# A decoder block in float32 on one core: the first feed-forward group rewoven with cross-attention steps and output tiles

## What is computed

```python
h = LN(x)                                   # causal self-attention, 16 heads of 32
s = (q @ k.T + slope * (key - query)) / sqrt(32)
s = 30 * tanh(s / 30)
x = x + softmax(causal(s)) @ v @ Wo.T + bo
h = LN(x)                                   # cross-attention, one head of 512
s = where(mask, h @ ctx.T / sqrt(512), -1e30)
x = x + softmax(s) @ ctx                    # zero for a batch entry without a valid token
h = LN(x)                                   # feed-forward, 512 -> 1536 -> 512
gate = silu(h @ fp8(gate_w) * gate_scale)
up = h @ fp8(up_w) * up_scale
x = x + (gate * up) @ fp8(down_w) * down_scale
```

## Time and profile before

| | us |
|---|---|
| median of 3 runs | 593.75 |
| lowest, highest | 592.24, 596.52 |
| the profiled execution | 594.02 |
| its span, first to last instruction | 592.3 |

### The profile page before, as it was taken

The page is one execution under the profiler, slowest core; times in us unless marked ns, Lnnn a source line. Parts: engine busy times, 40 slices in busy tenths (PEclk is TensorE's granted clock), DMA queues, the critical chain, the costliest instruction groups (busy, mean ns, idle before and its releaser), DMA issues.

```text
span 592.3 us, 9934 instructions
## 1 busy us (share of the span) xinstructions
PE 553.8 (94%) x3890; PEld 454.0 (77%) x3890; DVE 337.2 (57%) x674; ACT 242.6 (41%) x471; POOL 280.0 (47%) x284
## 2 busy tenths in 40 slices
PE   2998998999989999897779999999999999999997
PEld 2787786888768887686657888888888888888885
DVE  6578648874498645975637855335533456234322
ACT  3538863578534774435543343023320334023310
POOL 5657867846757458794665322013410243003320
PEclk9999998999999999998999999999999999999999
DMA  8862132532217220219562802000001000000001
GB/s 267 298 183 73 38 107 72 173 114 72 72 37 213 73 73 18 74 55 316 163 231 73 265 1 90 35 37 1 2 18 54 0 1 1 35 37 0 2 18 53
DMA packets 44189, 50.98 MB, mean 86 GB/s; under 512 B 3184, under 2 KB 25712, under 8 KB 44144
## 3 DMA queue, kind: packets, MB, share of 16 engines
q1 hardware_dynamic: 44144, 50.36, 26.0%
HBM read 36.72 MB, written 13.63 MB: 85 GB/s over the span
## 4 chain that ended last, share of the span: by engine, by line
PE 75%; POOL 10%; ACT 6%; DVE 5%; issue 2%; DMA 1%; SPq 0%; DVEq 0%; ACTq 0%
PE bank L262 49%; PE bank L396 15%; PE bank L257 3%; PE bank L318 2%; POOL probs L625 2%; PE bank L336 2%; POOL x_res L646 2%; PE bank L343 2%; POOL q_w L634 2%; POOL q_w L632 2%; PE bank L354 1%; DVE q_m L1060 1%; ACT probs L785 1%; POOL reduced L619 1%; ACT probs L780 1%
## 5 line engine op out<-in xcount | busy, mean ns | idle before, releaser
L262 PE MATMUL bank<-reduced 128*128 128x512 f32 x1536 | 363.0, 394 | 1.6 <-DVE reduced L990 1.6
L262 PEld LDWEIGHTS bank<-reduced 128*128 128x128 f32 x1536 | 287.5, 189 | 64.2 <-issue 3.6
L729 POOL TENSOR_TENSOR f_parts<-fused,f_parts 128x512 fp32r<-128x512 f32 x48 | 62.2, 1296 | 178.3 <-ACT f_parts L920 178.3
L902 ACT ACTIVATE tanh_g<-bank,half_gate 128x512 f32<-128x512 f32 x48 | 33.1, 690 | 156.0 <-PE bank L262 155.6
L396 PE MATMUL bank<-reduced,f_parts 128*128 128x512 f32 x384 | 88.7, 391 | 0.0
L396 PEld LDWEIGHTS bank<-reduced,f_parts 128*128 128x128 f32 x384 | 71.9, 188 | 15.3 <-issue 0.5
L625 POOL TENSOR_SCALAR_AFFINE_SELECT probs<-probs 128x512 f32<-128x512 f32 x64 | 41.6, 679 | 66.7 <-ACT probs L785 66.7
L1176 DVE SCALAR_TENSOR_TENSOR silu<-tanh_g,bank 128x512 f32<-128x512 f32 x48 | 32.9, 685 | 61.0 <-ACT tanh_g L902 61.0
L780 ACT ACTIVATE probs<-bank 128x512 f32<-128x512 f32 x64 | 33.0, 603 | 54.5 <-PE bank L318 51.7
L632 POOL TENSOR_TENSOR q_w<-q_w,q_m 128x512 f32<-128x512 f32 x36 | 47.2, 1310 | 3.1 <-DVE q_m L1062 3.1
L634 POOL TENSOR_TENSOR q_w<-q_w,q_m 128x512 f32<-128x512 f32 x36 | 47.2, 1310 | 2.8
(11 more groups left out here) (86 smaller groups left out, 537.0 us busy)
## 6 DMA issues: line engine op xcount, KB each, us to landing
quantized<-q_w SPq DMA_DIRECT2D x36, 256.0 KB, 3.3
reduced<-quantized SPq DMA_DIRECT2D x12, 512.0 KB, 7.8
memT_sb<-in_memT SPq DMA_DIRECT2D x16, 256.0 KB, 4.6
mem_sb<-in_mem SPq DMA_DIRECT2D x16, 256.0 KB, 5.6
out<-y_sb SPq DMA_DIRECT2D x16, 256.0 KB, 2.0
x_res<-in_x SPq DMA_DIRECT2D x3, 1024.0 KB, 6.8
q_w<-in_gate_w SPq DMA_DIRECT2D x12, 256.0 KB, 3.2
q_w<-in_up_w SPq DMA_DIRECT2D x12, 256.0 KB, 3.2
```

What stands on the lines that cost most here:

```text
L262: ins = pe.matmul(dst, stationary, moving, start=(n == 0), stop=(n == len(pairs) - 1))
L729: pool.tensor_tensor(f_lo[:, f, :], fused[:, f % 2, :], f_hi[:, f, :].bitcast(F32), ALU.subtract).then_inc(f_lo_ready, 1)
```

## The change

- PE: after slices 0 and 1 there is one loop over the slices 2 to 11. Each turn is a slice, a step of cross-attention (of group 2 until f = 6, of group 3 from f = 7) and, in turns 3 to 6, one output tile. Slice 1 goes into banks 5 and 3 instead of 4 and 5. In turns 4 to 7 the pair of banks is reversed, so that the up half takes the bank that the output tile of the turn before used. The last steps of cross(3, .) move between the halves of the down tiles; `down` can now do a part of its slices.
- DVE, ACT and POOL: the same loop. The late slabs (prepare 34, 35; round 33 to 35; flag 32 to 35) are spread over the turns, one a turn, behind `fuse`, `high` and `ffn_low`. `norm_moments` and `norm_apply` of group 3 follow right behind its last output tile.
- The flag sum goes to bank 5 instead of bank 7, and DVE adds it to `fuse_c` before its four `x_low`, not behind them.
- SyncE: in group 3 the first four `load_gate_up` come two slab steps earlier, followed by the loads of cross-attention's memory for group 2.

The diff, cut (in `down` and in the SyncE part all edits are shown):

```diff
-F_BANK = 7
+F_BANK = 5
...
             gate_up(0, 0, (0, 1))
             cross(G - 2, 0)
-            gate_up(0, 1, (4, 5))
+            gate_up(0, 1, (PT_BANK, RO_BANK))
             context(G - 1, 3)
             cross(G - 2, 1)
-            gate_up(0, 2, (0, 1))
-            cross(G - 2, 2)
-            gate_up(0, 3, (6, 7))
-            cross(G - 2, 3)
-            for i in range(GT):
-                wo_proj(G - 1, i, (0, 1, 6, 7)[i])
-                if i < GT - 1:
-                    cross(G - 2, 4 + i)
-            gate_up(0, 4, (0, 1))
-            gate_up(0, 5, (6, 7))
-            for k in range(6):
-                gate_up(0, 6 + k, ((0, 1), (6, 7))[k % 2])
-                cross(G - 1, k)
+            for f in range(2, FT):
+                pair = ((0, 1), (6, 7))[f % 2]
+                gate_up(0, f, pair[::-1] if 4 <= f < 8 else pair)
+                if f < 7:
+                    cross(G - 2, f)
+                else:
+                    cross(G - 1, f - 7)
+                if 3 <= f < 7:
+                    wo_proj(G - 1, f - 3, (6, 0)[f % 2])
...
-                        turn_x3(g + 1, i, (2, 4, 0, 1)[i] if g == 0 else i)
...
+                        turn_x3(g + 1, i, (2, 0, 1, 5)[i] if g == 0 else i)
+                if g == 0:
+
+                    down(0, 0, 6, 0, DOWN_FIRST)
+                    cross(G - 1, 5)
+                    down(0, 1, 7, 0, DOWN_FIRST)
+                    cross(G - 1, 6)
+                    down(0, 0, 6, DOWN_FIRST)
+                    down(0, 1, 7, DOWN_FIRST)
+                    down(0, 2, 2)
+                    down(0, 3, 4)
...
-                    if hg == 1 and g:
+                    slabs = slabs_at(ROUNDED, g, hg)
+                    if hg == 0 and g == G - 1:
+                        slab_steps(slabs[:2])
+                        slabs = slabs[2:]
+                        wait_filled(sp, ("V", g, GT - 1))
+                        for f in range(4):
+                            load_gate_up(f)
+                    if hg == (0 if g == G - 1 else 1) and g:
                         for i in range(GT):
                             load_memT(g - 1, i)
...
             ffn_low(0, 0)
+            low_part(G - 1, 3)
+            ffn_low(0, 1)
             flag_slabs(flagged[:1])
             round_slabs(late[:1])
...
+            for f in range(2, FT):
                 ffn_low(0, f)
-                if f == 7:
+                flag_slabs(flagged[f - 1:f])
+                round_slabs(late[f - 1:f])
+                if f == 6:
+                    norm_scale(1, G - 1)
...
+            for f in range(2, FT):
+                gate(0, f)
+                if f == 2:
+                    context_high(G - 1, 3)
+                if f < 7:
+                    cross(G - 2, f)
+                else:
+                    cross(G - 1, f - 7)
+                high(0, f)
+                flag_slabs(late[f - 2:f - 1])
...
             fuse(0, 0)
-            prepare_slabs(late[:1])
             fuse(0, 1)
             normalize_context(G - 1, 3)
             cross(G - 2, 1)
-            prepare_slabs(late[1:])
...
+            for f in range(2, FT):
+                fuse(0, f)
+                if f < 7:
+                    cross(G - 2, f)
+                else:
+                    cross(G - 1, f - 7)
+                if 3 <= f < 7:
+                    wo_out(G - 1, f - 3)
+                prepare_slabs(late[f - 2:f - 1])
+                if f == 6:
+                    norm_moments(1, G - 1)
+                    norm_apply(1, G - 1, G - 1)
```

More of the change, by code:

```diff
@@ L385, in turn_x3, with down @@
                 transposes(dst, xn2[:, i, :]).then_inc(done, 1)
-            def down(g, i, b):
-                dst, done = take(("D", g, i), b)
+            def down(g, i, b, first=0, last=FT):
+                if first == 0:
+                    take(("D", g, i), b)
+                dst, done = bank[b], filled[b]
                 t = slice(i * S, (i + 1) * S)
-                for f in range(FT):
+                for f in range(first, last):
                     if i == 0:
@@ L473, in _ @@
                     for i in range(GT):
[L474 to L478 removed]
+                        turn_x3(g + 1, i, (2, 0, 1, 5)[i] if g == 0 else i)
[9 more added lines that the diff above has]
+                else:
+                    for i in range(GT):
+                        down(g, i, 4 + i)
         @block.sync
@@ L563, in _ @@
                             load_mem(g - 1, i)
-                    if g == G - 1 and hg == 1:
-                        wait_filled(sp, ("V", g, GT - 1))
-                        for f in range(4):
-                            load_gate_up(f)
                     if g == G - 1 and hg == 3:
@@ L1145, in _ @@
                 prepare_slabs(slabs_at(PREPARED, g, 2))
-                for i in range(GT):
-                    x_low(g + 1, i)
                 if g == G - 1:
@@ L1153, in _ @@
                     wait_drained(dve, ("F",))
+                for i in range(GT):
+                    x_low(g + 1, i)
                 normalize_context(g, 2)
```

70 lines of the change are left out of this document (12 added, 58 removed).

## The result

| | before | after |
|---|---|---|
| median (6 runs each) | 593.71 us | 581.14 us |
| lowest, highest | 592.24, 596.88 | 578.59, 583.00 |
| the profiled execution | 594.02 | 580.64 |
| its span | 592.3 | 578.9 |

After over before is 0.977 (95% interval 0.975 to 0.980). The medians are 12.6 us apart; the spans of the two profiled executions 13.4 us.

The account below looks back on a forecast made before the run. PE's work was taken as the floor, so only its idle or low-clock time could go: 2.35 + 1.26 + 3.50 + 4.19 + 1.6 = 12.9 us gained, 0.3 given back, 594.0 - 12.6 = 581.4 us; range 578.5 to 588.0.

Parts of the forecast that it names:

- the clock terms: Time at low clock won back behind two stops: 1.26 us at context(3, 2), 1.6 us behind cross(2, 2)'s turned probabilities.
- What bounds the kernel: PE's work is the floor; some 10 us of its idle time lie in the stretch's first 51 us.
- Term 1: Flag in bank 5, added first: the 2.35 us stop ahead of context(3, 2) goes, plus 1.26 us of clock.
- Term 2: Scores of cross(2, 1): slice 1 leaves bank 4 and the slab goes behind slice 2; all 3.50 us go.
- Term 3: Turned probabilities of cross(2, 2): the exp comes in time, so 4.19 us go, plus 1.6 us of clock.
- The new waits: Waits the new turns add on PE: 0.2 to 0.3 us at group 3's norm, nothing at the other places listed.
- ring through POOL: In turns 2 to 4 POOL's four instructions take 5.2 us; the slice held back is 16 us away: no wait.
- Rival A: One stop forms anew, 2 to 3 us plus 1.6 us of clock: 585.4 us; chance 0.20 with the flag's failure.
- B: The stops only change place, about 3 us in each of turns 3 to 6: 593.4 us; chance 0.08.
- C: POOL and DVE hold each other up, 5.3 us in turns 3 to 5 plus clock falls: 602 us; chance 0.04.
- The clock's rule: Half rate is TensorE's default and activity releases it; with the stops gone no clock fall is left.
- the rows alone: Judged by the profile's rows, a clock fall could come in the same place without the stop; 1.3 us would stay.

Follow-up runs that it names:

- the change again: The changed kernel itself, unaltered, measured once more as a yardstick: 580.74 us, ratio to before 0.976.
- the early flag in bank 7: The changed kernel with the flag sum back in bank 7, DVE's addition still ahead of the four `x_low`: 581.50 us, ratio to before 0.979.
- all but the turns: Before plus flag, SyncE and the late slabs' new orders on DVE, POOL and ACT; PE's order and slice and tile banks as before: 582.74 us, 0.981.

## Why the prediction was right, and where it was not

The time is right: 581.14 us for 581.4 forecast, the span 578.9 for 579.7, and the stretch lost 13.22 us for 12.6. That is a little more than the 13.1 that the prediction called the most that can be won; the clock terms are why. Step by step:

- **What bounds the kernel.** Right: PE's stops and its clock in the stretch were what moved. What lies behind the second group's start kept its length (203.8 us).
- **Term 1, 2.35 + 1.26 us.** The size is right (the context took 1.88 us where it had taken 3.21, so 1.33 of clock). Its cause was told wrong by half. The sum gives it to the flag's edit, and of SyncE's part it says "PE waits for none of them now, so nothing". That step failed. With the flag alone the stop moves to slice 0's weights (0.56 us won), and SyncE's part is what keeps it away (3.62 us when undone). The price was hidden by the very stop that was to go. The sum was not spoilt only because both parts are in the change, and together they give what it had for one. That this term came out is luck and no reading of the loads.
- **Term 2, 3.50 us.** Right, and by the two causes that were named, DVE's queue and slice 1's bank: the stop needs both. In the full change the banks are worth nothing beside the slab's place (0.03 us).
- **Term 3, 4.19 + 1.6 us.** Right. The exp ended at 288.99 (forecast 289.1), PE asked at 290.50 (forecast 290.9), and the cross step behind it took 1.36 us (290.50 to 291.86) for 2.98, so 1.62 of clock. DVE's slab is behind terms 2 and 3, shown both ways: DVE's slabs moved alone win 6.10 us, and slab 34 put back costs 4.92, which is term 3 only, since slice 1 stays out of bank 4.
- **The clock terms were too small**, 2.86 us against 3.37. The fall before 311.29 us reached into the output tile behind it (3.06 us for twelve matmuls, for which the prediction took 2.82 elsewhere), some 0.2 to 0.3 us that were not counted.
- **The new waits.** The norm, 0.2 to 0.3 us forecast, was 0.23. Up halves, ring through POOL, loads of slices 4 to 11, down tiles: nothing, as said. The output tile of turn 6 was drained from 323.71 on (forecast 324.4), and PE was done with slice 7 at 327.3 (forecast 328.1).
- **The turns, POOL and ACT.** The prediction gave no share of the gain to them. The runs do: without POOL's new order a stop of 1.96 us comes, without ACT's one of 2.44, without the turns one of 1.30. Each of these stops forms only once the slabs on DVE have moved, so these edits keep the gains of terms 2 and 3 from being lost again. None of them was tried alone on before. Rival A ("one stop forms anew") describes each of these kernels, only not the full change.
- **Rivals B and C.** The argument against B was DVE's work in a turn, "5.5 to 7.5 us", below PE's 8.4. Its own terms give up to 5.5 + 2.8 = 8.3, which would have left no margin. The margin was there all the same: DVE was busy for 6.9 us from its silu of turn 3 to that of turn 4, with slab 35 among it, and for 5.0 in the next turn, where DVE has no slab any more. There was no stop in turns 3 to 6. C did not come: POOL's mean for a low half stayed at 1295 ns (1296), and DVE's instructions that read a bank kept 0.69 and 0.75 us with POOL busy.
- **The clock's rule.** With the stops gone no fall was left in the stretch (1.00), so the 1.3 us that "the rows alone" left open did not stay.

The line of the page for POOL's low halves, to be held beside the earlier trace rows:

```profile
L742 POOL TENSOR_TENSOR f_parts<-fused,f_parts 128x512 fp32r<-128x512 f32 x48 | 62.2, 1295 | 174.8 <-ACT f_parts L929 174.8
```

The parts don't add up to one ledger. Undone one at a time, flag 3.95, SyncE 3.62, slab 34 on DVE 4.92, turns 1.55: 14.0 us, with POOL's and ACT's orders not counted, for a change of 13.22. From before upward the same parts begin with 0.56. That is how covers look: the flag's edit is worth 3.95 us as the last one made and 0.56 as the first.

## What to carry to other kernels

When a stop goes, ask of every resource that is used shortly behind it when it really arrived: no wait in the trace names a load that landed while PE stood for something else, and it is next in line. When an item has a step on several engines, go through all of them before moving it on one, and look on each for what stands queued behind its wait, since a pair of cheap instructions (2.8 us) that must wait 4.1 us for another engine holds up all that is queued behind it. And undo parts in the full change as well as adding them to the old kernel: only the two together tell an edit that wins time from one that guards it.

## What the runs showed of the hardware

- **The same program, another clock.** PE stands about 2.2 us at about 95 us. There the clock fell in some executions and not in others: from 90 to 100 us it was 1.00 in the first profile of the change and in the change again, with the flag undone and with slab 34 back, and 0.79 to 0.85 with SyncE undone, slice 1 in banks 4 and 5, the early flag in bank 7 and all but the turns; up to there all of them have the same program. The flag's product came between 269.8 and 273.7 us after the start; the mean clock up to it was 1.00 in the four earliest of them (269.8 to 270.6) and 0.98 or 0.99 in the others. A fall is not ordered by the length of the stop either: slice 0 ran slow behind stops of 1.84 and 2.01 us, while before had 1.00 from 286 to 298 us around its stop of 3.50; a stop of 3.50 us in before with flag and SyncE had 0.50 from 286 to 290. The Trainium skill (TensorE: Matmul & The Clock Gate, Part 1: The HAM clock gate) says that the monitor runs free of the kernel's start, so that one kernel shows different numbers of slow matmuls from run to run. The Trainium skill tells this of a kernel's start; the runs show it in the middle of one, by the clocks above. A clock term taken from one execution, as the 1.26 and 1.6 us here, is therefore a likely value and not a fixed one.
- **A tiny DVE instruction can take six times as long beside POOL.** The product of 128x1 by 128x1 (`x_w`) takes 0.16 us with POOL idle, in the changed kernel at 321.00, and 1.03 beside POOL's rounding at 313.64. It ends at 314.67, POOL's instruction at 314.66:

```profile
313.64 1.03 DVE L1034 TENSOR_TENSOR x_w<-x_rec,valid 128x1 f32<-128x1 f32 x1
...
321.00 0.16 DVE L1034 TENSOR_TENSOR x_w<-x_rec,valid 128x1 f32<-128x1 f32 x1
...
313.36 1.30 POOL L647 TENSOR_TENSOR q_w<-q_w,q_m 128x512 f32<-128x512 f32 x1
```

Its neighbours that read a bank did not change. The Trainium skill (SBUF — State Buffer, Who interferes with whom) says that a VectorE instruction with two inputs in SBUF contends with a GpSimd instruction that reads SBUF, and names no exception for a small one; the rows agree. The prediction had weighed this rule for slabs and `xn` only and counted the rest of a turn as reading a bank, which this instruction does not. In the chain that led to the stop of 1.30 us above it took 1.05 us instead of 0.16, so some 0.9 us of that stop are put down to it, by these rows and not by a run of its own.
